# Gated-delta attention block on one Trainium2 core: the sums of squares of the queries are made once, from queries read back from DRAM during the inverse, and no longer in each recurrence unit

## The chip, the cores and the metric

The kernel runs on one core of one Trainium2 chip. The metric is the device time of one execution in microseconds (us). The engines are TensorE (PE, with its weight loads PEld), VectorE (DVE), ScalarE (ACT), GpSimd (POOL) and SyncE (SP), which here only issues transfers. Each engine works through its own instructions in order, and they are tied together by semaphores.

## The reference

The block is a modulated layer norm, a gated delta rule over 4 sequences of 512 tokens with 6 heads (key size 64, value size 128), a gated output norm and projection, and then a modulated feed-forward part. What matters for the change is cut out here:

```python
def short_conv(x, w):
    K = w.shape[1]
    xp = jnp.pad(x, ((0, 0), (K - 1, 0), (0, 0)))
    y = sum((xp[:, i:i + x.shape[1], :] * w[:, i] for i in range(K)))
    return jax.nn.silu(y)

def l2norm(x):
    return x * jax.lax.rsqrt(jnp.sum(x * x, -1, keepdims=True))

def _step(S, xs):
    qt, kt, vt, gt, bt = xs
    S = S * jnp.exp(gt)[..., None, None]
    pred = jnp.einsum('bhk,bhkv->bhv', kt, S)
    delta = (vt - pred) * bt[..., None]
    S = S + jnp.einsum('bhk,bhv->bhkv', kt, delta)
    return (S, jnp.einsum('bhk,bhkv->bhv', qt, S))
...
q = l2norm(q) * dk ** (-0.5)
k = l2norm(k)
...
o = o * jax.lax.rsqrt(jnp.mean(o * o, -1, keepdims=True) + EPS) * norm_weight
o = o * jax.nn.silu(gate)
```

The length of a query scales one row of `o`, and `o` is normalised afterwards. So the kernel leaves the queries as they are and adds their sum of squares, times 128 x EPS x 64, to the sum of squares of `o` before the root: this is the only place where the query's norm is used.

## The kernel before

The program is a list of steps (`plan`), built by plain Python; each engine then walks the list and issues its own part of each step. So the place of a step in the list sets the order on all five engines.

1. **Norms and the keys' projections** (to about 95 us). x is normed, turned and modulated into Hhi and Hlo (a value and its rest, for products of three matmuls each), and the decay, beta and key projections are made. The keys' sums of squares are made here: squares on ACT (`k2_square`), six matmuls with the selector `pick` for each half (`k2`, line 1121), a turn by PE, and further steps.
2. **Projections with the inverse beside them** (to about 340 us). 15 weight tiles in the order of `tile_seq`, each for 4 batches, make 60 slots. A slot issues one projection ahead (12 matmuls of 512 columns, four PSUM banks in turn). Tiles 0 to 2 are the queries, 3 to 8 the values: for these ACT scales the projection into one of two buffers Y (`conv_in`, line 1417), DVE adds three taps of the short convolution (`conv_tap`, line 1707), ACT applies SiLU into one of three buffers O (`conv_out`, line 1422), and SP stores the tile to the DRAM tensor `scrU` (`store_u`, line 933). Tiles 9 to 14 are the gates: ACT alone takes them to O (`gate`, line 1427). Beside the slots run three lanes of side work: one makes the matrices to be inverted (`inverse_1`) and later merges them, one does the 31 steps of the inverse on DVE (`inverse_2`: a multiply and an add for each, lines 1797 and 1800; two of these instructions in a convolution's slot, three in a gate's), one the late modulation rows. Side work that needs PSUM uses two pairs of banks in turn (`take`, `pfree`). POOL clears the four parts of P (`clear_p`, line 2016) for the inverse's results, which `inv2_back` loads at 275 us. P is 48 KB of each partition, in four parts: the first is used earlier for the products of `inv_gm`, the second and third by the inverse, the fourth for squares of keys.
3. **Recurrence** (to about 560 us). 16 units (a chunk of 64 tokens of two batches, 6 heads). A slot holds the recurrence of unit u, the preparation of u + 1, and the post-work of u - 1 and u - 2 (`slot_of`, line 650). SP loads the unit's queries and values from `scrU` into one of two buffers U. PE's order in a slot is `rec_x`, `pr_tr`, `pr_exp`, `rec_d`, `po_tr`, `pr_kq`, `rec_q`, `rec_s`, `rec_o`, `rec_v`, `po_wo`. POOL squares the unit's queries (line 2048, into Q2), PE sums them over the 64 rows of a head at the end of `pr_kq` (line 1227), DVE scales the sums into QN (line 1844), and the post-work adds QN to the squares of `o` (line 1879).
4. **Feed-forward part** (to the end), nearly all PE.

Three lines of the part that goes:

```python
for m in range(3):
    t = mm(bank(4 + 2 * p)[:, 192 + 2 * m:194 + 2 * m], Q2[:, m, :], halves, False, True)
t.then_inc(sem("pr_kq"), 1)
```

## Time and profile before

| | us |
|---|---|
| median of 3 runs | 1142.64 |
| lowest and highest run | 1140.72, 1145.05 |
| profiled execution, its own time | 1141.11 |
| its span in the trace | 1139.3 |
| PE busy | 1066.0 (94%) |
| DVE busy | 619.6 (54%) |
| ACT busy | 371.8 (33%) |
| POOL busy | 228.3 (20%) |

Read the busy shares as averages over stages with different limits. The granted clock of PE was 0.971 of full speed over the span. PE's busy time counts records that overlap, so the time that an instruction takes on PE is read from the distance of starts, not from its own length.

### The profile page before, as it was taken

To read this page: it belongs to the slowest core of one execution; us is meant where nothing else is said; L and a number is where in the kernel's file an instruction comes from. 1 tells how busy PE (TensorE), PEld (TensorE's weight loads), DVE (VectorE), ACT (ScalarE), POOL (GpSimd) and SP (SyncE) were. 2 spreads that over 40 slices of the span, in tenths; PEclk is the share of its full clock that TensorE was granted. 3 is DMA by queue.
4 is the path that set the end of the run, shared out by engine and by line. 5 is a ranking of instruction groups with operands and counts; after the bars stand their busy time and mean duration, and the time that the engine had idled before them with its cause. 6 is when DMAs were issued, how large, how long until landed. Compare 5 with 4: busy or idle time off the path is not lost.

```text
span 1139.3 us, 18747 instructions
## 1 busy us (share of the span) xinstructions
PE 1066.0 (94%) x7396; PEld 863.5 (76%) x7396; DVE 619.6 (54%) x994; ACT 371.8 (33%) x670; POOL 228.3 (20%) x182
## 2 busy tenths in 40 slices
PE   4898989988998999999978999999999999999998
PEld 2685667767776888888756788788888888888886
DVE  3766445998864677776645433333343334325356
ACT  4575465324435333343236112121121211212110
POOL 1322110001014555555331000000000000004092
PEclk8899999999898999999979999999999999999999
DMA  5503326338328455665622101001010000101222
GB/s 192 193 10 102 80 63 166 94 96 200 85 74 196 95 129 126 154 154 126 191 69 65 56 1 38 18 1 56 1 56 1 28 28 1 56 1 65 67 82 110
DMA packets 147350, 94.72 MB, mean 83 GB/s; under 512 B 93376, under 2 KB 124352, under 8 KB 147136
## 3 DMA queue, kind: packets, MB, share of 16 engines
...
## 4 chain that ended last, share of the span: by engine, by line
PE 79%; DVE 9%; ACT 5%; issue 4%; DMA 1%; POOL 1%; SPq 0%; DVEq 0%; ACTq 0%; POOLq 0%
PE ps L1051 75%; ACT t L1351 5%; PE ps L1059 3%; DVE t L1615 3%; DVE t L1707 3%; PE ps L1239 1%; DVE t L1620 1%; DMA t<-in_x 1%; POOL t L2081 1%; DMA t<-scrU 0%; ACT L1373 0%; DVE t L1807 0%; DMA t<-in_wf 0%; DVE t L1625 0%; DVE t L1818 0%
## 5 line engine op out<-in xcount | busy, mean ns | idle before, releaser
L1051 PE MATMUL ps<-t,t 128*128 128x512 f32 (+6 forms) x6528 | 1009.2, 337 | 55.4 <-DMA t<-in_wmod 8.7
L1051 PEld LDWEIGHTS ps<-t,t 128*128 128x128 f32 (+3 forms) x6528 | 803.5, 168 | 237.1 <-issue 43.1
L1615 DVE TENSOR_TENSOR t<-ps,t 128x512 f32<-128x512 f32 (+4 forms) x306 | 209.2, 701 | 255.0 <-PE ps L1051 243.1
L1351 ACT ACTIVATE t<-t 128x512 fp32r<-128x512 f32 (+7 forms) x330 | 185.0, 578 | 340.8 <-DVE t L1615 201.6
L1615 DVE TENSOR_TENSOR t<-t,t 128x512 fp32r<-128x512 f32 (+16 forms) x209 | 161.9, 779 | 116.6 <-ACT t L1351 109.5
L1351 ACT ACTIVATE t<-ps 128x512 f32<-128x512 f32 (+4 forms) x193 | 108.3, 566 | 329.8 <-PE ps L1051 317.0
L2089 POOL TENSOR_TENSOR t<-t,t 128x512 f32<-128x512 f32 x16 | 22.3, 1392 | 404.6 <-DVE t L1615 402.5
L1707 DVE SCALAR_TENSOR_TENSOR t<-ps,t,t 128x511 f32<-128x511 f32 (+2 forms) x108 | 80.4, 747 | 19.8 <-ACT t L1351 17.0
L1059 PE MATMUL ps<-t,t 128*128 128x128 f32 (+1 forms) x388 | 60.9, 292 | 11.9 <-DVE t L1620 8.9
L1351 ACT ACTIVATE t<-ps,t 128x512 f32<-128x512 f32 (+2 forms) x96 | 56.9, 621 | 33.3 <-DVE t L1615 10.7
L1059 PEld LDWEIGHTS ps<-t,t 128*128 128x128 f32 (+1 forms) x388 | 45.8, 149 | 28.0 <-DVE t L1620 12.8
L2069 POOL TENSOR_TENSOR t<-t,t 128x768 fp32r<-128x768 f32 x16 | 29.1, 1817 | 38.9 <-ACT t L1351 38.6
L2016 POOL MEMSET t<- 128x3072 f32 x4 | 10.7, 2666 | 123.0 <-DVE t L1615 92.9
L2092 POOL TENSOR_TENSOR t<-t,t 128x512 f32<-128x512 f32 x16 | 23.5, 1468 | 41.0 <-DMA t<-scrX 39.0
L1993 POOL TENSOR_TENSOR t<-t,t 128x512 fp32r<-128x512 f32 x16 | 21.2, 1324 | 50.9 <-ACT t L1351 49.1
L2075 POOL TENSOR_TENSOR t<-t,t 128x512 f32<-128x512 f32 x16 | 20.5, 1280 | 50.4 <-DVE t L1615 50.3
L1625 DVE BATCH_NORM_STATS2 t<-t 128x6 f32<-128x512 f32 x32 | 22.1, 690 | 13.2 <-DMA t<-in_x 8.4
L1351 ACT ACTIVATE t<-t,t 128x1 f32<-128x1 f32 (+2 forms) x36 | 13.2, 366 | 48.8 <-DVE t L1627 48.7
L2004 POOL TENSOR_TENSOR t<-t,t 128x384 f32<-128x384 f32 x16 | 14.0, 872 | 57.6 <-PE ps L1051 38.2
L1695 DVE SCALAR_TENSOR_TENSOR t<-ps,t,t 128x510 f32<-128x510 f32 (+1 forms) x24 | 17.9, 744 | 12.4 <-ACT t L1351 11.9
L2061 POOL TENSOR_TENSOR t<-t,t 128x768 f32<-128x768 f32 x16 | 23.6, 1474 | 2.7 <-POOL t L2075 2.4
L1620 DVE TENSOR_SCALAR t<-t,t,t 128x512 f32<-128x512 f32 x32 | 20.6, 645 | 0.6 <-ACT t L1351 0.6
...
## 6 DMA issues: line engine op xcount, KB each, us to landing
...
t<-in_x SPq DMA_DIRECT2D x32, 128.0 KB, 2.8
```

The source lines that it names most:

```text
L1051: return e.matmul(o, l, r_, start=start, stop=stop, skip_group_check=True)
L1059: return e.transpose(o, i, idn)
L1351: return e.activation(o, i, f, **kw)
L1615: return e.tensor_tensor(o, a, b, op)
L1620: return e.tensor_scalar(o, a, s1, s2, o1, o2)
L1625: e.bn_stats(st6[:, slot_, :], src).then_inc(sem(name + "bn"), 1)
L1707: e.scalar_tensor_tensor(yy[:, d + 1:SEQ], p_[:, 0:SEQ - d - 1], cwt[:, j, 2 - d:3 - d], yy[:, d + 1:SEQ], ALU.mult, ALU.add).then_inc(sem ...
L1993: signal(e.tensor_tensor(Hlo[:, b, k, :], HF[k][:, :], Hhi[:, b, k, :].bitcast(f32), ALU.subtract), "p_lo")
L2061: signal(e.tensor_tensor(heads(Sg[:, :, :]), heads(S[:, 6 * pp:6 * pp + 6, :]), bc(decay, 3, [128, 2, 3, 128]), ALU.mult), "p_sg")
L2069: signal(e.tensor_tensor(OZl[:, :, :], OZ[:, :, :], OZh[:, :, :].bitcast(f32), ALU.subtract), "p_ozl")
L2089: signal(e.tensor_tensor(ya(b, s), ya(b, s), gbB[:, b, :], ALU.mult), "p_out")
L2092: signal(e.tensor_tensor(ya(b, s), ya(b, s), xo(b, s), ALU.add), "p_out")
```

## The change

A fourth lane, `q_norms`, starts in slot 21 (the second slot of the sixth tile, after the last query tile has been given to the store). In that slot SP gets twelve loads, one for each of 3 query tiles and 4 batches, from `scrU` into places in the first and the fourth part of P (QS, QQ), and POOL two squares of 128 x 3072 in place. Three slots later, in slot 24, PE sums them with `pick` in twelve matmuls into four strips of one bank (`q_sum`) and ACT copies the bank to SBUF; in slot 25 PE turns the sums in sixteen small matmuls (`q_turn`) and ACT scales them into `q_eps` in eight instructions; in slot 26 POOL clears the fourth and the first part of P, which it did before in the ninth step of the inverse. `q_eps` is the tile of `beta`, whose last reader is over by then. Q2, QN, the square, the three matmuls and the scaling in each unit are gone. `inv2_back` waits for the clears by their new numbers.

```diff
--- before.py
+++ after.py
@@ -129,6 +129,10 @@
     tmp = A_.new([128, 768])
     K2 = [at(P_at[3] + i * 6144, [128, 3, 512]) for i in range(2)] + [A_.new([128, 3, 512])]
     kq = tmp[:, 0:512]
+    QS = [at(P_at[3], [128, 6, SEQ]), at(P_at[0], [128, 6, SEQ])]
+    QQ = [[QS[0][:, g_, :] for g_ in range(4)], [QS[1][:, g_, :] for g_ in range(4)],
+          [QS[g_ // 2][:, 4 + g_ % 2, :] for g_ in range(4)]]
+    qsum, q_eps = QQ[0][0], beta
     IG = [at(P_at[0] + i * 1536, [128, H, 64]) for i in range(8)]
     assert A_.p <= 229216, A_.p
 
@@ -168,8 +172,7 @@
     UG = [B_.new([128, H, 128]) for _ in range(2)]
     O2, OS, OZ = (B_.new([128, H, 128]) for _ in range(3))
     OZh, OZl = B_.new([128, H, 128], f32r), B_.new([128, H, 128], f32r)
-    Q2 = B_.new([128, 3, 128])
-    QN, ssq = B_.new([128, 2, H]), B_.new([128, 2, H])
+    ssq = B_.new([128, 2, H])
     rso = B_.new([128, H])
     XB = [B_.new([128, D]) for _ in range(2)]
     Woh = B_.new([128, H, D], f32r)
@@ -464,27 +467,46 @@
             made["kk"] = u + 1
             yield
 
+    cleared = {}
+
+    def clear(s):
+        step("clear_p", s=s)
+        cleared[s] = tick("p_pz")
+
+    def q_norms():
+        step("q_square")
+        yield
+        yield
+        yield
+        p, free = take()
+        step("q_sum", bank=4 + 2 * p, free=free)
+        pfree(p, ("a_k2c", 3))
+        yield
+        p, free = take()
+        step("q_turn", p=p, free=free)
+        pfree(p, ("a_k2", 3))
+        yield
+        clear(3)
+        clear(0)
+
     def inverse_2():
         yield
         step("inv2_load")
         for _ in range(4):
             yield
         for i in range(31):
-            if i == 8:
-                step("clear_p", s=3)
-                step("clear_p", s=0)
             step("inv2_mul", i=i)
             yield
             step("inv2_add", i=i)
             yield
-        step("clear_p", s=1)
+        clear(1)
         yield
         step("inv2_store")
-        step("clear_p", s=2)
+        clear(2)
         for _ in range(3):
             yield
         for s in range(4):
-            step("inv2_back", s=s)
+            step("inv2_back", s=s, cleared=cleared[s])
         for _ in range(3):
             yield
         made["inverse"] = 1
@@ -505,8 +527,8 @@
               (4, 2, inverse_1(3)), (0, 2, merge(0), "inverse", 1), (0, 2, merge(1)), (0, 2, merge(2)),
               (0, 2, merge(3))],
              [(0, 3, inverse_2(), "kk", 16)],
-             [(0, 1, late_mods())]]
-    running, left = [None] * 3, [0] * 3
+             [(0, 1, late_mods())], [(21, 1, q_norms())]]
+    running, left = [None] * 4, [0] * 4
     slot = 0
 
     def due(lane, now):
@@ -615,12 +637,12 @@
                 late_out.append((y, tap, tile, b))
             if n == 14:
                 start_b(b)
-            for l in (2, 0, 1):
+            for l in (2, 3, 0, 1):
                 side(l)
             slot += 1
     while any(running) or any(lanes):
         begin(99)
-        for l in range(3):
+        for l in range(4):
             side(l)
     n_proj = count["proj"]
     step("table", set="natural_log_exp_and_others")
@@ -948,6 +970,14 @@
                 blocks = scrA.rearrange("s b t i -> (s b) t i")
                 for i in range(3):
                     e.dma_start(nAp[:, i, :, :], blocks[128 * i:128 * i + 128]).then_inc(sem("d_nap"), 16)
+            elif kind == "q_square":
+                e.wait_ge(sem("inv_g"), 16)
+                e.wait_ge(sem("k2"), 2)
+                for m in range(3):
+                    for b in range(4):
+                        e.wait_ge(*at_least(stored[(m, b)]))
+                        src = scrU.rearrange("(s b) p j t -> b j p s t", b=4)[b, m]
+                        e.dma_start(QQ[m][b].rearrange("p (s t) -> p s t", s=4), src).then_inc(sem("d_cT"), 16)
             elif kind == "inv2_store":
                 e.wait_ge(sem("v_i2a"), 31)
                 blocks = scrP.rearrange("s b c t -> (s b) c t")
@@ -956,7 +986,7 @@
             elif kind == "inv2_back":
                 s = st["s"]
                 e.wait_ge(sem("d_pp"), 48)
-                e.wait_ge(sem("p_pz"), (2, 3, 4, 1)[s])
+                e.wait_ge(*at_least(st["cleared"]))
                 for k in range(4):
                     q = slice(32 * k, 32 * k + 32)
                     e.dma_start(P[q, s, :, q],
@@ -1126,6 +1156,21 @@
                 e.wait_ge(sem("a_k2c"), 2)
                 for i in range(4):
                     t = tr(bank(st["bank"])[:, 128 * i:128 * i + 128], kq[:, 128 * i:128 * i + 128], ident)
+                t.then_inc(sem("k2"), 1)
+            elif kind == "q_sum":
+                e.wait_ge(*at_least(st["free"]))
+                e.wait_ge(sem("p_q2"), 2)
+                for m in range(3):
+                    for g_ in range(4):
+                        t = mm(bank(st["bank"])[32 * g_:32 * g_ + 32, :], pick[:, m, :], QQ[m][g_], m == 0, m == 2)
+                t.then_inc(sem("k2"), 1)
+            elif kind == "q_turn":
+                e.wait_ge(*at_least(st["free"]))
+                e.wait_ge(sem("a_k2c"), 3)
+                for c in range(8):
+                    for half in range(2):
+                        t = mm(PSt[64 * half:64 * half + 64, 4 + 2 * st["p"] + c // 4, c % 4 * 128:c % 4 * 128 + 128],
+                               qsum[:, 64 * c:64 * c + 64], ident, c % 4 == 0, True)
                 t.then_inc(sem("k2"), 1)
             elif kind == "sums":
                 bk = bank(4 + 2 * st["p"])
@@ -1220,11 +1265,8 @@
                     for half in range(2):
                         for par in range(2):
                             q = slice(64 * par, 64 * par + 64)
-                            mm(PSt[64 * half:64 * half + 64, 4 + 2 * p + par, m * 64:m * 64 + 64],
-                               kcols(u)[q, m, 64 * half:64 * half + 64], U[u % 2][q, m, 64 * half:64 * half + 64], m == 0, True)
-                e.wait_ge(sem("p_q2"), u + 1)
-                for m in range(3):
-                    t = mm(bank(4 + 2 * p)[:, 192 + 2 * m:194 + 2 * m], Q2[:, m, :], halves, False, True)
+                            t = mm(PSt[64 * half:64 * half + 64, 4 + 2 * p + par, m * 64:m * 64 + 64],
+                                   kcols(u)[q, m, 64 * half:64 * half + 64], U[u % 2][q, m, 64 * half:64 * half + 64], m == 0, True)
                 t.then_inc(sem("pr_kq"), 1)
             elif kind == "rec_v":
                 u = st["u"]
@@ -1457,6 +1499,21 @@
                 rows = slice(64 * half, 64 * half + 64)
                 e.wait_ge(sem("k2"), half + 1)
                 act(kq[rows, :], bank(st["bank"])[rows, :], ACT.Copy).then_inc(sem("a_k2c"), 1)
+            elif kind == "q_sum":
+                e.wait_ge(sem("k2"), 4)
+                act(qsum, bank(st["bank"]), ACT.Copy).then_inc(sem("a_k2c"), 1)
+            elif kind == "q_turn":
+                e.wait_ge(sem("k2"), 5)
+                e.wait_ge(sem("v_br"), 1)
+                src = PSt[:, 4 + 2 * st["p"]:6 + 2 * st["p"], :].rearrange("p b (i c g m a) -> p g c (b i) a m", i=2, c=2, g=4, a=2)
+                dst = q_eps[:, :, :].rearrange("p (s v c) (a m) -> p v c s a m", s=4, v=2, a=2)
+                for half in range(2):
+                    rows = slice(64 * half, 64 * half + 64)
+                    for v_ in range(2):
+                        for c in range(2):
+                            t = act(dst[rows, v_, c], src[rows, 2 * v_ + half, c, :, :, 0:3], ACT.Copy,
+                                    scale=128.0 * EPS * DK)
+                t.then_inc(sem("a_k2"), 1)
             elif kind == "k2_log":
                 e.wait_ge(sem("v_k2"), 4)
                 act(z2[:, :, :], kq2[:, :, :], ACT.Ln).then_inc(sem("a_k2"), 1)
@@ -1839,11 +1896,6 @@
             elif kind == "pr_kq":
                 u, p = st["u"], st["p"]
                 e.wait_ge(sem("pr_kq"), u + 1)
-                if u >= 2:
-                    e.wait_ge(sem("v_ms"), u - 1)
-                e.tensor_scalar(QN[:, u % 2, :].rearrange("p (a m) -> p m a", a=2),
-                                bank(4 + 2 * p)[:, 192:198].rearrange("p (m a) -> p m a", a=2), 128.0 * EPS * DK, None,
-                                ALU.mult).then_inc(sem("v_qn"), 1)
                 e.wait_ge(sem("a_pexp"), u + 1)
                 if u >= 2:
                     e.wait_ge(sem("rec_o"), u - 1)
@@ -1875,8 +1927,8 @@
                     e.wait_ge(sem("a_pn"), 2 * u - 2)
                 e.tensor_reduce(ssq[:, u % 2, :], O2[:, :, :], mybir.AxisListType.X, ALU.add).then_inc(sem("v_red"), 1)
                 e.wait_ge(sem("v_red"), u + 1)
-                e.wait_ge(sem("v_qn"), u + 1)
-                tt(ssq[:, u % 2, :], ssq[:, u % 2, :], QN[:, u % 2, :], ALU.add).then_inc(sem("v_ms"), 1)
+                e.wait_ge(sem("a_k2"), 3)
+                tt(ssq[:, u % 2, :], ssq[:, u % 2, :], q_eps[:, u, :], ALU.add).then_inc(sem("v_ms"), 1)
             elif kind == "po_os":
                 u = st["u"]
                 e.wait_ge(sem("a_pn"), 2 * u + 2)
@@ -2002,16 +2054,19 @@
                 sh = [128, H, 64]
                 in_order()
                 signal(e.tensor_tensor(IG[u % 8][:, :, :], bc(later, 1, sh), bc(g[:, u, :], 2, sh), ALU.mult), "p_ig")
+            elif kind == "q_square":
+                e.wait_ge(sem("d_cT"), 16 + 12 * 16)
+                for q_ in QS:
+                    in_order()
+                    signal(e.tensor_tensor(q_[:, :, :], q_[:, :, :], q_[:, :, :], ALU.mult), "p_q2")
             elif kind == "clear_p":
                 s = st["s"]
-                if s == 0:
-                    e.wait_ge(sem("inv_g"), 16)
-                elif s == 1:
+                if s == 1:
                     e.wait_ge(sem("v_i2m"), 31)
                 elif s == 2:
                     e.wait_ge(sem("d_pp"), 48)
                 else:
-                    e.wait_ge(sem("k2"), 2)
+                    e.wait_ge(sem("k2"), 5)
                 in_order()
                 signal(e.memset(P[:, s, :, :], 0.0), "p_pz")
             elif kind == "clear_b":
@@ -2041,11 +2096,6 @@
                                        ALU.mult), "p_gm")
                 in_order()
                 signal(e.tensor_tensor(GMl[:, :, :], bc(within, 1, sh), bc(glo[:, u, :], 2, sh), ALU.mult), "p_gm")
-                e.wait_ge(sem(f"d_u{u % 2}"), 32 * (u // 2 + 1))
-                if u:
-                    e.wait_ge(sem("pr_kq"), u)
-                in_order()
-                signal(e.tensor_tensor(Q2[:, :, :], U[u % 2][:, 0:3, :], U[u % 2][:, 0:3, :], ALU.mult), "p_q2")
             elif kind == "rec_x":
                 u = st["u"]
                 pp = place(u)[0]
```

PE in the recurrence, the end of one slot's middle part. Before (t94 is a buffer U, t25 the keys kT, t1 the constants, t114 Q2, t89 the state S):

```order
1394 L1051 MATMUL ps<-t94_142,t25_73 64x64 [waits d_u1,v_prep]
1395 L1051 MATMUL ps<-t94_142,t25_73 64x64 x11
1396 L1051 MATMUL ps<-t1_49,t114_162 128x2 [waits p_q2]
1397 L1051 MATMUL ps<-t1_49,t114_162 128x2 x2
1398 L1051 MATMUL ps<-t89_137,t100_148 64x128 [waits v_os]
```

and with the change (t96 is U, t91 S):

```order
1387 L1081 MATMUL ps<-t96_144,t25_73 64x64 [waits d_u1,v_prep]
1388 L1081 MATMUL ps<-t96_144,t25_73 64x64 x11
1389 L1081 MATMUL ps<-t91_139,t102_150 64x128 [waits v_os]
```

The three matmuls on the squares and PE's wait for POOL's square (p_q2) are gone; nothing else in the slot moved.

ACT in slots 23 to 26 of the projections. Before (t37 to t39 are the buffers O, t35 and t36 the buffers Y, t32 a weight tile's upper part, t31 the next one's):

```order
203 L1351 ACTIVATE t39_87<-ps 128x512 [waits proj,d_scrU2]
204 L1351 ACTIVATE t32_80<-t30_78 128x512 [waits d_w1,proj]
205 L1351 ACTIVATE t35_83<-ps,t2_50 128x512 [waits a_cout,proj]
206 L1351 ACTIVATE t36_84<-ps,t2_50 128x512 [waits a_cout,proj]
207 L1351 ACTIVATE t37_85<-t35_83 128x512 [waits v_tap,d_scrU0]
208 L1351 ACTIVATE t35_83<-ps,t2_50 128x512 [waits a_cout,proj]
```

and with the change (t55 is the first of the squared tiles, whose first 512 columns take the sums, t9 is `q_eps`):

```order
205 L1393 ACTIVATE t35_83<-ps,t2_50 128x512 [waits a_cout,proj]
206 L1393 ACTIVATE t55_103<-ps 128x512 [waits k2]
207 L1393 ACTIVATE t36_84<-ps,t2_50 128x512 [waits a_cout,proj]
208 L1393 ACTIVATE t37_85<-t35_83 128x512 [waits v_tap,d_scrU0]
209 L1393 ACTIVATE t9_57<-ps 64x4x6 [waits v_br,k2]
210 L1393 ACTIVATE t9_57<-ps 64x4x6 x7
211 L1393 ACTIVATE t35_83<-ps,t2_50 128x512 [waits a_cout,proj]
```

The copy of the sums stands between the scalings (`conv_in`) of slots 24 and 25, the eight small instructions before that of slot 26.

SP after the change, from the slot before the lane starts (t56 is the second squared tile):

```order
98 L955 DMA scrU<-t39_87 128x4x128 [waits a_gate]
99 L955 DMA scrU<-t37_85 128x4x128 [waits a_gate]
100 L980 DMA t55_103<-scrU 128x4x128 [waits d_scrU0,k2,inv_g]
```

and after ten more loads:

```order
111 L980 DMA t56_104<-scrU 128x4x128 [waits d_scrU1]
112 L955 DMA scrU<-t38_86 128x4x128 [waits a_gate]
113 L955 DMA scrU<-t39_87 128x4x128 [waits a_gate]
114 L923 DMA t30_78<-in_W1 128x512 [waits v_wlo]
```

The stores 112 and 113 and the weight load 114 stood right behind 99.

## Rows read from the trace of the kernel before

**Rows 1.** The page, the chain that ended last, by engine.
```profile
PE 79%; DVE 9%; ACT 5%; issue 4%; DMA 1%; POOL 1%; SPq 0%; DVEq 0%; ACTq 0%; POOLq 0%
```

**Rows 2.** Busy us of PE, PEld, DVE, ACT, POOL by stretch; PE clock, DMA share, GB/s.
```profile
200.00:250.00 50.00, 44.20 (x190) 34.98 (x189) 48.51 (x64) 16.54 (x28) 0.00 (x0) 1.00 0.35 100
400.00:450.00 50.00, 50.00 (x603) 43.20 (x596) 34.39 (x58) 16.33 (x38) 26.56 (x23) 1.00 0.55 125
```

**Rows 3.** Order of time, PE in one unit: start us, us, engine, operation.
```profile
467.10 0.19 PEld L1051 LDWEIGHTS ps<-t,t 128*128 128x128 f32 x1
...
467.65 0.19 PEld L1051 LDWEIGHTS ps<-t,t 128*128 128x128 f32 x1
...
471.35 0.48 PE L1051 MATMUL ps<-t,t 128*128 128x512 f32 x1
```

**Rows 4.** The chain that ended last, in order of time: start us, us, what.
```profile
452.95 4.28 PE ps L1051 x90
...
466.66 4.27 PE ps L1051 x90
```

**Rows 5.** Order of time, POOL in the same unit.
```profile
468.61 1.82 POOL L2069 TENSOR_TENSOR t<-t,t 128x768 fp32r<-128x768 f32 x1 [2.79 <-ACT t L1351]
```

**Rows 6.** Groups by line and form: count, busy us, mean ns, idle before.
```profile
L2061 POOL TENSOR_TENSOR t<-t,t 128x768 f32<-128x768 f32 x16 | 23.6, 1474 | 2.7 <-POOL t L2075 2.4 <-POOL t L2048 0.2 <-POOL t L2030 0.2
...
L2016 POOL MEMSET t<- 128x3072 f32 x4 | 10.7, 2666 | 123.0 <-DVE t L1615 92.9 <-PE ps L1051 25.5 <-DMA scrP<-t 4.2
...
L1844 DVE TENSOR_SCALAR t<-ps 128x6 f32<-128x6 f32 x16 | 2.7, 167 | 8.6 <-PE ps L1051 8.6
```

**Rows 7.** Order of time, start of the recurrence, three engines.
```profile
362.05 0.83 POOL L2048 TENSOR_TENSOR t<-t 128x384 f32<-128x384 f32 x1 [5.54 <-DMA t<-scrU]
...
363.02 2.38 POOL L2030 TENSOR_TENSOR t<-t,t 128x1024 fp32r<-128x1024 f32 x1
...
364.00 1.41 DVE L1615 TENSOR_TENSOR t<-t,t 128x6 f32<-128x6 f32 x1
...
366.34 0.94 PE L1051 MATMUL ps<-t,t 128*128 128x128 f32 x6 [1.07 <-DVE t L1615]
```

**Rows 8.** Order of time, SP's queue: the third of the five stores.
```profile
202.40 0.67 SPq L933 DMA_DIRECT2D scrU<-t  x1
```

**Rows 9.** Order of time, ACT in slots 22 to 25.
```profile
204.47 0.60 ACT L1351 ACTIVATE t<-ps 128x512 f32<-128x512 f32 x1 [3.22 <-DMA scrU<-t]
205.26 0.60 ACT L1351 ACTIVATE t<-ps 128x512 f32<-128x512 f32 x1 [0.19 <-DMA scrU<-t]
...
209.16 0.69 ACT L1351 ACTIVATE t<-ps,t 128x512 f32<-128x512 f32 x1 [2.03 <-PE ps L1051]
```

**Rows 10.** DMA from 200 to 212 us, in 40 slices of 0.3 us.
```profile
GB/s 0 0 0 0 0 0 55 102 143 273 360 347 341 343 353 331 329 350 167 7 266 282 287 294 290 282 41 0 0 0 0 0 0 0 0 0 82 116 239 416
```

**Rows 11.** Order of time, PE: a modulation row, and a sum of keys' squares.
```profile
15.19 1.94 PE L1051 MATMUL ps<-t,t 128*32 128x512 f32 x8
...
85.43 2.77 PE L1051 MATMUL ps<-t,t 128*32 128x512 f32 x12
```

**Rows 12.** PE by the microsecond: length, busy, clock, DMA share, GB/s.
```profile
277.00:278.00 1.00, 0.41 (x2) 1.00 1.25 244
...
280.00:281.00 1.00, 0.00 (x0) 0.71 1.27 138
...
287.00:288.00 1.00, 1.00 (x5) 0.88 1.06 166
```

**Rows 13.** Order of time, slots 24 to 31: DVE, and PE's projections.
```profile
212.02 1.72 DVE L1615 TENSOR_TENSOR t<-t,t 128x660 f32<-128x660 f32 x2
...
213.65 2.31 DVE L1707 SCALAR_TENSOR_TENSOR t<-ps,t,t 128x511 f32<-128x511 f32 x3
...
223.94 13.92 PE L1051 MATMUL ps<-t,t 128*128 128x512 f32 x60 [0.96 <-DVE t L1707]
```

**Rows 14.** Groups by line and form: ACT's copies of merged blocks.
```profile
L1351 ACT ACTIVATE t<-ps 32x192 f32<-32x192 f32 x32 | 10.3, 321 | 31.6 <-PE ps L1051 31.2
```

## The prediction

> **What bounds the kernel now.** I read the chain first, then the stages, then the order of time at the two places that the change touches. The chain that ended last runs on TensorE (PE) for 79% of the span and on DVE for 9% [rows 1]. The reader is to see that this average hides two kinds of stage [rows 2]. From 400 to 450 us, in the recurrence, PE has 50.00 busy us in 50 and DVE 34.39: each PE instruction there is paid in full. From 200 to 250 us, where the projections run beside the inverse, DVE has 48.51 of 50 and PE 44.20: DVE sets the pace, and PE, ACT and POOL have slack only as long as none of them makes DVE wait. The change takes work out of the first and puts work, and waits, into the second.
>
> **What is removed.** In each unit PE sums the squares with three products (two records each) right after the 64x64 products of `pr_kq`. The first of their weight loads begins at 467.10 and the last, the sixth, at 467.65 [rows 3]: 0.11 us apart, so the next work could begin at 467.76. That is 0.66 us a unit. The groups of PE work return every 13.7 us (452.95, 466.66 [rows 4]), with PE never idle. Fifteen units in PE-bound slots give 15 x 0.66 = 9.9 us; the sixteenth, in the prologue, I cost at nothing and keep for the range.
>
> Does the next wait take it back? The nearest is that of `po_wo`, which starts at 471.35 [rows 3] and needs POOL's subtraction, 468.61 + 1.82 = 470.43 [rows 5]. The start moves to 470.69, and 0.26 us is left. So I expect the slot to shrink by the whole 0.66.
>
> POOL loses 16 squares of 0.83 us or more and DVE 16 scalings on 6 columns of 0.17 [rows 6]. Neither bounds a steady slot, so both cost nothing there. At the start it is different. A DVE add on as few columns took 1.41 us from 364.00 and ended with a POOL subtraction for Wo (363.02 to 365.40), and PE stood 1.07 us for DVE right after [rows 7]. POOL came that late because the square of unit 2 stood ahead of it, from 362.05 after 5.54 us of waiting for its queries. Without the square I take 1.1 us as gained (bounds 0 and 2). All that is gained: 11.0 us, from 9 to 13.
>
> The Trainium skill says of such a row, in "SBUF — State Buffer", section "Who interferes with whom", that a DVE instruction with two SBUF inputs and a GpSimd instruction that reads SBUF exclude each other for a whole instruction. By that rule the new squares would block steps of the inverse on DVE; by the times below DVE is already standing when the first square starts, so the sum stays as it is by row and rule alike, and were they to meet, the loss would be larger, not smaller.
>
> **What is added, step by step.** On SP twelve loads of 256 KB (3.1 MB) come between the third and the fourth of the five stores that now go out from 201.37.
>
> - *Issue.* The third store is issued at 202.40 and takes the queue 0.67 [rows 8]: the loads are issued from 203.07. What they wait for has happened by then, except the last query tile's store, which is the first of the three.
> - *Transfer.* The first two stores' landings let ACT go at 204.47 and 205.26 [rows 9]: 0.79 us for 256 KB, in the same pieces of 512 bytes, while up to 360 GB/s flow [rows 10]. The third lands at about 206.05, and twelve more at 0.79 make 9.5: 215.5. Bounds: 211.9, if only issue at some 0.57 each and 2 us to landing count; 216.8, at the 290 GB/s of the lower slices.
> - *Squares.* POOL starts when all twelve are in. It takes 0.83 us for 384 columns of the same operation, 1.47 for 768 and 2.38 for 1024 of others [rows 6, 7]: 2.16, 1.92 and 2.32 ns a column. Two squares of 3072 columns are 13.3 us at 2.16 (bounds 11.8 and 14.3). Ready at 228.8.
> - *`q_sum` on PE* stands behind slot 25's projection, which ends at 209.1, where ACT stops waiting for it [rows 9]. PE, in order, then stands until 228.8. Twelve products in four column strips follow. The six of a `k2` sum, in two strips, take 2.77 us, the four of a modulation row, in four strips, 1.94 [rows 11]: 0.46 and 0.48 each. Twelve make 5.5 (lower bound 2.8, if four strips go as fast as two).
> - *The clock.* PE went idle at 277.4; by 281 the granted clock had fallen from 1.00 to 0.50 (from 2.4 to 1.2 GHz), and it came back in the slice 287 to 288, some six microseconds after work had resumed [rows 12]. After 20 us of idle I expect the same: the first 6 us do 3 us of work. `q_sum` ends at 228.8 + 6 + 2.5 = 237.3.
> - *ACT* has the copy of the sums in its order ahead of the scaling that opens slot 25's convolution: 0.60 and 0.69 [rows 9] make 238.6. DVE needs that scaling at 213.65; before it stand only slot 24's taps and one step of the inverse [rows 13]. DVE waits 25.0 us.
> - *`q_turn`*, a slot later: PE's next projection, twelve products at 0.23 [rows 13], 2.8; sixteen products at 0.16, 2.5 (three full ones, as six records, take 0.94 [rows 7], and here two halves of the columns can share); eight small ACT instructions at 0.24, 1.9 (0.32 for 192 columns [rows 14], here 24); the next scaling, 0.7. 237.3 + 7.9 = 245.2. DVE would want it at 238.6 + 2.31 + 1.72 = 242.6. Another 2.6 us, from 0 to 4.
>
> Together DVE is 27.6 us later. Nothing absorbs it: DVE has no idle to give in this stage, the inverse stands behind the taps in DVE's own order, and PE is held by the same wait, so it can't run ahead. The stores behind the loads go out some 3 us late; the first buffer that they free is asked for at 216 in the old order, and if that cover fails it falls inside the long wait. POOL's clears of P now wait for `q_turn`, but the loads into P come at 275. Both cost nothing.
>
> For strips the Trainium skill ("TensorE: Matmul & The Clock Gate", "Why this matters for your kernels") gives a speed-up of 3.07 for four small tiles with different rows of the array and of 2.38 for three with different columns. By the latter, and 0.92 us a product in one strip, twelve would take 12 x 0.92 / 2.38 = 4.6 us, an estimate, and the sum would end 0.9 lower. I keep 5.5, since the row with four strips shows 0.48 a product.
>
> **Sum.** 27.6 - 11.0 = +16.6 us on the profiled execution's 1141.11: 1157.7, told as 1158. The median of the runs shown is 1142.64, 1.5 above that execution, and they spread over 4.3 us; the range covers it. About 0.5% (5.7 us) is what a measurement of this kernel can tell from no change.
>
> **Rivals.**
> - *The stall is hidden: faster.* With loads and squares done before DVE comes to 213.65 only the gain is left, 1130. Sum, clock and both ACT steps need at least 5.5 + 1.3, so the squares would have to end by 206.8, 3.7 us after the first load is issued. It decides there, and the DMA rows alone speak against it. Chance 0.04, with a half hidden one in it.
> - *The stall is short: no change.* POOL may run long instructions faster per column; its clears write 3072 columns in 2.67 us [rows 6]. At that pace both squares take 5.3, and at the other lower bounds the wait is 211.9 + 5.3 + 5.5 + 1.3 - 213.65 = 10.4 against a gain of 11: 1140.5, and 1143.5 with `q_sum` at 8.5. Against it: a clear reads nothing, and three operations that read agree on 1.9 to 2.3 ns. Chance 0.06.
> - *The gain fails: slower still.* `po_wo` has only 0.26 us left. If semaphores take more, PE waits there, and a gain under half leaves 1141.1 + 27.6 - 5 = 1164, or 1169 with none. Against it: POOL's subtraction hangs on `po_tr`, which does not move. Chance 0.10.
> - *Forecast*: full stall, full gain, 0.80.
>
> **How the numbers follow.** The low end of the stall is 211.9 + 11.8 + 5.5 + 1.3 - 213.65 = 16.9 with no second wait, and with a gain of 13 gives +4. The high end is 216.8 + 14.3 + 8.9 + 1.3 - 213.65 = 27.7 and a second wait of 4, with a gain of 9: +23. All at one end is rare; 8 in 10 reach from +7 to +26, the lower part of the failing gain among them: 1148 to 1167. Slower by over 0.5% holds the forecast and the failing gain, 0.90; within 0.5% the short stall, 0.06; faster 0.04.
>
> **What would show it.** Right: a hole on DVE and PE between about 210 and 238 us, ended by POOL's squares and then by ACT; two POOL instructions of about 6.6 us from 215; a clock of 0.50 behind the hole; slots of 13.0 us in place of 13.7, PE still at 50 of 50. Wrong: squares under 4 us each; a hole under 11 us; DVE time won back before 340, so that the recurrence starts less than 20 us later than now; slots that stay at 13.7, with PE waiting for POOL before `po_wo`.

## The result, and the profile after

The changed kernel takes 1151.11 us in the median of four runs (1149.09 to 1151.85), the kernel before, on the same chip, 1143.79 (1140.72 to 1145.05): a ratio of 1.0059, 95% interval 1.004 to 1.0078. It is **slower, by 0.6% or 7.3 us**. The direction was forecast and the median lies in the stated range, near its lower end; the size was not: +16.6 us forecast, less than half of it found. The profiled execution took 1149.09 us with a span of 1147.3, against 1141.11 and 1139.3.

The page of the changed kernel, the chain that ended last, by engine:

```profile
PE 74%; DVE 10%; ACT 6%; issue 4%; DMA 3%; POOL 2%; SPq 2%; DVEq 0%; ACTq 0%; POOLq 0%
```

PE has 5 points less of the chain than in [rows 1], and DMA, POOL and SP's queue, which were at 1, 1 and 0, now have 3, 2 and 2: the chain runs through the loads and the squares. The same two stretches as in [rows 2] (busy us of PE, PEld, DVE, ACT and POOL, then PE's clock, DMA share and GB/s), after:

```profile
200.00:250.00 50.00, 31.05 (x162) 22.36 (x161) 26.81 (x39) 11.20 (x26) 15.95 (x4) 0.80 0.44 116
400.00:450.00 50.00, 50.00 (x622) 43.25 (x621) 38.78 (x59) 18.33 (x40) 24.94 (x20) 1.00 0.56 126
```

Beside the inverse DVE lost 21.70 of its 48.51 busy us, and PE 13.15 of 44.20 (at a granted clock of 0.80, where it was 1.00). In the recurrence PE is full in both kernels, but does more of its instructions in the same time (622 against 603).

**The hole.** Order of time of the changed kernel, slots 24 to 26 (start us, us, engine, line, operation, and in brackets the idle time before it with what ended it). After the change the helpers' lines are L1081 for a product, L1393 for an ACT instruction, L1764 for the taps of a convolution and L1672 for the other DVE work:

```profile
203.64 10.04 SPq L980 DMA_DIRECT2D t<-scrU  x12
...
210.24 2.31 DVE L1764 SCALAR_TENSOR_TENSOR t<-ps,t,t 128x511 f32<-128x511 f32 x3
...
212.47 1.72 DVE L1672 TENSOR_TENSOR t<-t,t 128x660 f32<-128x660 f32 x2
...
218.29 10.69 POOL L2061 TENSOR_TENSOR t<-t 128x3072 f32<-128x3072 f32 x2 [73.22 <-DMA t<-scrU]
...
229.12 33.14 PE L1081 MATMUL ps<-t,t 128*32 128x512 f32 x170 [18.95 <-POOL t L2061]
...
234.10 0.60 ACT L1393 ACTIVATE t<-ps 128x512 f32<-128x512 f32 x1 [25.92 <-PE ps L1081]
...
235.31 2.32 DVE L1764 SCALAR_TENSOR_TENSOR t<-ps,t,t 128x511 f32<-128x511 f32 x3 [21.12 <-ACT t L1393]
...
238.97 0.85 ACT L1393 ACTIVATE t<-ps 64x24 f32<-64x24 f32 x8 [3.17 <-PE ps L1081]
239.84 0.69 ACT L1393 ACTIVATE t<-ps,t 128x512 f32<-128x512 f32 x1
...
240.56 2.32 DVE L1764 SCALAR_TENSOR_TENSOR t<-ps,t,t 128x511 f32<-128x511 f32 x3 [1.23 <-ACT t L1393]
```

Read down the brackets. POOL waited for the loads, PE 18.95 us for POOL, ACT 25.92 for PE, DVE 21.12 for ACT: one relay of four engines, each with its whole queue behind it. Slot 25's taps start at 235.31, where they started at 213.65 in [rows 13]; slot 26 adds a second, small wait of 1.23.

**Where it is given back.** Executions differ by some us in the stages before 210 us, so I compare distances between the same instructions. Four landmarks of the kernel before (slot 24's taps start at 209.79 in it), in order of time, are POOL's clear at the end of the merge and the fourth and sixteenth sum over a unit's squares in the recurrence:

```profile
331.80 1.38 POOL L2021 MEMSET t<- 128x1536 f32 x1 [54.08 <-PE ps L1051]
...
403.71 0.95 DVE L1876 TENSOR_REDUCE t<-t 128x6 f32<-128x768 f32 x1 [0.55 <-ACT t L1351]
...
566.15 0.94 DVE L1876 TENSOR_REDUCE t<-t 128x6 f32<-128x768 f32 x1
```

The same instructions of the changed kernel:

```profile
353.74 1.38 POOL L2076 MEMSET t<- 128x1536 f32 x1 [53.03 <-PE ps L1081]
...
421.55 0.95 DVE L1928 TENSOR_REDUCE t<-t 128x6 f32<-128x768 f32 x1
...
575.01 0.94 DVE L1928 TENSOR_REDUCE t<-t 128x6 f32<-128x768 f32 x1
```

| stretch | before, us | after, us | difference |
|---|---|---|---|
| slot 24's taps to the merge's last clear | 122.01 | 143.50 | +21.5 |
| that clear to the 4th sum (start of the recurrence) | 71.91 | 67.81 | -4.1 |
| 4th to 16th sum (steady slots) | 162.44 | 153.46 | -9.0 |
| all three | 356.36 | 364.77 | +8.4 |

Slot 24's taps start 0.45 us later than before in this pair, and 0.9 us is won behind the sixteenth sum; with these the span's +8.0 is complete. That last 0.9 may be chance: act_here below, with the same recurrence and the same end, takes 3.9 us longer than the change from there on.

### The profile page after: what moved, and what is told of

Its sections match the earlier page's. It is cut to its first block, busy times and chain, and to the rows that moved or that the text cites. A ratio compares the mean times of both kernels' runs of the same rounds, so it can differ in the third digit from the quotient of the medians.

```text
span 1147.3 us, 18633 instructions
## 1 busy us (share of the span) xinstructions
PE 1058.9 (92%) x7356; PEld 852.8 (74%) x7356; DVE 623.6 (54%) x978; ACT 372.1 (32%) x679; POOL 221.7 (19%) x168
## 4 chain that ended last, share of the span: by engine, by line
PE 74%; DVE 10%; ACT 6%; issue 4%; DMA 3%; POOL 2%; SPq 2%; DVEq 0%; ACTq 0%; POOLq 0%
PE ps L1081 70%; ACT t L1393 5%; DVE t L1672 4%; PE ps L1089 3%; DVE t L1764 3%; POOL t L2061 1%; PE ps L1281 1%; DMA t<-scrU 1%; DVE t L1677 1%; DMA t<-in_x 1%; POOL t L2131 1%; DMA t<-scrA 1%; ACT L1415 1%; SPq L980 1%; POOL t L2119 0%
## 5 line engine op out<-in xcount | busy, mean ns | idle before, releaser
L1081 PE MATMUL ps<-t,t 128*128 128x512 f32 (+5 forms) x6488 | 1001.2, 340 | 69.8 <-POOL t L2061 19.0
L1081 PEld LDWEIGHTS ps<-t,t 128*128 128x128 f32 (+3 forms) x6488 | 792.2, 167 | 254.9 <-issue 69.7
L1672 DVE TENSOR_TENSOR t<-ps,t 128x512 f32<-128x512 f32 (+4 forms) x306 | 208.2, 700 | 254.9 <-PE ps L1081 242.7
L1393 ACT ACTIVATE t<-t 128x512 fp32r<-128x512 f32 (+7 forms) x330 | 184.6, 577 | 329.1 <-DVE t L1672 202.3
L1393 ACT ACTIVATE t<-ps 128x512 f32<-128x512 f32 (+5 forms) x202 | 109.6, 551 | 352.8 <-PE ps L1081 339.9
L1672 DVE TENSOR_TENSOR t<-t,t 128x512 fp32r<-128x512 f32 (+16 forms) x209 | 162.3, 781 | 113.5 <-ACT t L1393 104.6
L1764 DVE SCALAR_TENSOR_TENSOR t<-ps,t,t 128x511 f32<-128x511 f32 (+2 forms) x108 | 80.4, 747 | 42.2 <-ACT t L1393 39.4
L1393 ACT ACTIVATE t<-ps,t 128x512 f32<-128x512 f32 (+2 forms) x96 | 56.8, 620 | 35.8 <-DVE t L1672 10.2
L2045 POOL TENSOR_TENSOR t<-t,t 128x512 fp32r<-128x512 f32 x16 | 21.2, 1326 | 51.9 <-ACT t L1393 50.2
L1393 ACT ACTIVATE t<-t,t 128x1 f32<-128x1 f32 (+2 forms) x36 | 13.2, 366 | 42.6 <-DVE t L1684 42.5
L1677 DVE TENSOR_SCALAR t<-t,t,t 128x512 f32<-128x512 f32 x32 | 26.3, 823 | 0.6 <-ACT t L1393 0.6
L2061 POOL TENSOR_TENSOR t<-t 128x3072 f32<-128x3072 f32 x2 | 10.6, 5306 | 73.3 <-DMA t<-scrU 73.2
L1752 DVE SCALAR_TENSOR_TENSOR t<-ps,t,t 128x510 f32<-128x510 f32 (+1 forms) x24 | 17.9, 744 | 12.4 <-ACT t L1393 11.8
```

The lines of the kernel that those rows point to most:

```text
L1081: return e.matmul(o, l, r_, start=start, stop=stop, skip_group_check=True)
L1393: return e.activation(o, i, f, **kw)
L1672: return e.tensor_tensor(o, a, b, op)
L1677: return e.tensor_scalar(o, a, s1, s2, o1, o2)
L1764: e.scalar_tensor_tensor(yy[:, d + 1:SEQ], p_[:, 0:SEQ - d - 1], cwt[:, j, 2 - d:3 - d], yy[:, d + 1:SEQ], ALU.mult, ALU.add).then_inc(sem ...
L2061: signal(e.tensor_tensor(q_[:, :, :], q_[:, :, :], q_[:, :, :], ALU.mult), "p_q2")
```

## The experiments

Each was run beside the kernel before on the same chip; ratios are to that kernel, with 95% intervals. The **main theory**: the time is the wait of slot 25 on the relay loads, squares, sum, copy, less the work that the recurrence no longer does, and the two add. Its main **rival**: something else of the change costs or gives, such as the DMA traffic, the moved memory, or a wait that a shorter slot uncovers. Lines left out of a diff are marked `...` or told below it.

### added_only: the change, with each unit's own squares and sums put back

```diff
+                e.wait_ge(sem("p_qu"), u + 1)
+                for m in range(3):
+                    t = mm(bank(4 + 2 * p)[:, 192 + 2 * m:194 + 2 * m], Q2[:, m, :], halves, False, True)
...
+                signal(e.tensor_tensor(Q2[:, :, :], U[u % 2][:, 0:3, :], U[u % 2][:, 0:3, :], ALU.mult), "p_qu")
```

> The change with the squares, the three sums and the scaling of each unit put back in the recurrence (the result of the new sums is computed and not used). Theory A, the wait at q_sum is the whole loss and it is passed on in full: the recurrence starts about 22 us later than in the kernel before, as in the change, and the time is 22 to 23 us above it (about 1165). Rival B, a good part of the hole is won back by slack before the end: under 15 us above it.

### gain_only: the kernel before, without the units' squares, sums and scalings

```diff
-                e.wait_ge(sem("p_q2"), u + 1)
-                for m in range(3):
-                    t = mm(bank(4 + 2 * p)[:, 192 + 2 * m:194 + 2 * m], Q2[:, m, :], halves, False, True)
...
-                signal(e.tensor_tensor(Q2[:, :, :], U[u % 2][:, 0:3, :], U[u % 2][:, 0:3, :], ALU.mult), "p_q2")
...
-                tt(ssq[:, u % 2, :], ssq[:, u % 2, :], QN[:, u % 2, :], ALU.add).then_inc(sem("v_ms"), 1)
+                tt(ssq[:, u % 2, :], ssq[:, u % 2, :], beta[:, u, :], ALU.add).then_inc(sem("v_ms"), 1)
```

> The kernel before without the unit's squares, sums and scaling, and nothing in their place: the output norm adds beta where the queries' sums belong. Theory A: the slot shrinks from 13.71 to 12.92 us as in the change, and with the start of the recurrence the time is 12 to 15 us below the kernel before (about 1129). Rival B, the change's slot was shorter for another reason (other placement of loads): the slot stays above 13.1 and the gain is under 9 us. Together with added_only: by A the two differences sum to that of the change, +7 to +8.

Measured: added_only 1164.45 us (1162.6 to 1168.79), ratio 1.0177 (1.014 to 1.0214), so +20.9 over the 1143.57 of the kernel before (22 to 23 were expected). gain_only 1128.14 us (1125.58 to 1133.45), ratio 0.986 (0.9821 to 0.99), so -15.4 (12 to 15 expected). Together +5.5, against the change's +7.3. The slot is 13.71 us in added_only, as before, and 12.92 in gain_only, as in the change. So the two halves add up to within two us, and the change is the difference of two larger effects, each with the sign that was forecast. The added half was overrated by 7 us (27.6 against 20.9), the removed one underrated by 4 (11.0 against 15.4). Part of those 15.4 is PE's clock: in the trace of gain_only, which is of its fastest run, it doesn't fall at the start of the recurrence, where it falls in the kernel before and in the change (rows further down).

### act_here: the change, with the squares on ACT, where POOL had them

```diff
         step("q_square")
-        yield
-        yield
-        yield
+        for _ in range(3):
+            yield
+        step("q_asq", i=0, n=12)
...
+            elif kind == "q_asq":
+                e.wait_ge(sem("d_cT"), 16 + 12 * 16)
+                for i in range(st["i"], st["i"] + st["n"]):
+                    q_ = QS[i // 6][:, i % 6, :]
+                    act(q_, q_, ACT.Square).then_inc(sem("a_q2"), 1)
```

(PE then waits for these twelve, and POOL has no squares.)

> The change with the squares on ACT, all twelve at once in slot 24 right before q_sum, nothing moved later. Theory: the hole is a serial sum of loads (until 218 us), squares, products and copies; ACT needs 12 x 0.6 = 7.2 us for the squares against POOL's 10.7, so the hole is 3.5 us shorter and the time 3 to 4 us below the change (about 1147). Rival: if the hole were set by something else than the end of the squares, the time stays at 1151.

Measured: 1146.27 us (1143.71 to 1151.69, ten runs), ratio 1.0028 (1.0009 to 1.0046). Order of time in it, the same places:

```profile
220.08 6.34 ACT L1393 ACTIVATE t<-t 128x512 f32<-128x512 f32 x12 [10.52 <-DMA t<-scrU]
...
226.57 13.73 PE L1081 MATMUL ps<-t,t 128*32 128x512 f32 x85 [15.79 <-ACT t L1393]
...
232.65 2.32 DVE L1769 SCALAR_TENSOR_TENSOR t<-ps,t,t 128x511 f32<-128x511 f32 x3 [16.38 <-ACT t L1393]
```

The squares take 6.34 us in place of 10.69, and DVE waits 16.38 us in place of 21.12: a link of the relay made 4.35 us shorter makes the wait 4.7 shorter. The time follows: the three stretches of the ledger sum to 360.06 us against the change's 364.77, 4.7 less. The medians stand 4.8 apart (the means 3.6, the runs of each kernel spread over up to 8), and the 1147 us expected was met. The squares' link is paid in full; the others were not varied.

### late12: the change, with the sum nine slots later

```diff
-        yield
-        yield
-        yield
+        for _ in range(12):
+            yield
         p, free = take()
         step("q_sum", bank=4 + 2 * p, free=free)
```

> The change with q_sum, q_turn and the two clears nine slots later (slots 33 to 35), loads and squares where they are. Theory A, only the wait cost: the hole at 210 to 235 is gone, and the time is 12 to 15 us below the kernel before (about 1129). Rival C, the squares of 5.3 us and the inverse's steps exclude each other on the port that POOL and DVE share (as the 1.41 us add of 6 columns did): single steps of the inverse on DVE take up to 5.3 us longer while a square runs, some 5 to 10 us in all, and the time is about 1135 to 1140. Rival D, the loads themselves hold up the stores: ACT waits for DMA before 220, several microseconds more than in the kernel before.

Measured: 1138.75 us (1134.42 to 1143.61, ten runs), ratio 0.9951 (0.9933 to 0.9969). The wait at slot 25 is gone, and yet not all of it comes back: from slot 24's taps to the merge's last clear it takes 133.31 us, 11.3 more than before. Theory A's 1129 us was missed, and rival C's 1135 to 1140 was met. (The profiled execution is the slowest of the ten, so its distances are read and not its end.) Order of time of late12:

```profile
222.00 11.24 POOL L2060 TENSOR_TENSOR t<-t 128x3072 f32<-128x3072 f32 x2 [76.30 <-DMA t<-scrU]
...
222.56 11.45 DVE L1671 TENSOR_TENSOR t<-t,t 128x720 f32<-128x720 f32 x2
...
233.93 2.30 DVE L1763 SCALAR_TENSOR_TENSOR t<-ps,t,t 128x511 f32<-128x511 f32 x3
```

The same two steps of the inverse in the kernel before:

```profile
219.81 1.84 DVE L1615 TENSOR_TENSOR t<-t,t 128x720 f32<-128x720 f32 x2
```

DVE's row counts as busy, but two steps that take 1.84 us take 11.45, just as long as POOL's two squares beside them: 9.6 us of the 11.3 lost without a wait in any list (the other 1.7 were not followed). This is what the Trainium skill describes in "SBUF — State Buffer", section "Who interferes with whom", for a DVE instruction with two SBUF inputs and a GpSimd instruction that reads SBUF, and this trace agrees. In the change itself DVE was standing already, as the prediction had it.

### late12_pieces: late12, with twelve squares of 512 columns

```diff
                 for q_ in QS:
-                    in_order()
-                    signal(e.tensor_tensor(q_[:, :, :], q_[:, :, :], q_[:, :, :], ALU.mult), "p_q2")
+                    for i in range(6):
+                        in_order()
+                        signal(e.tensor_tensor(q_[:, i, :], q_[:, i, :], q_[:, i, :], ALU.mult), "p_q2")
```

> As late12, with the two squares of 3072 columns cut into twelve of 512. Theory A: as late12. Rival C: a step of the inverse now waits for at most one piece of about 0.9 us, so this one is 3 to 8 us faster than late12. Should the squares get slower in pieces (a fixed cost for each), nothing waits for them before slot 33.

Measured: 1134.68 us (1133.2 to 1139.14), ratio 0.9921 (0.9892 to 0.995), 4.1 below late12, inside the 3 to 8 of rival C. Order of time:

```profile
221.76 17.66 POOL L2061 TENSOR_TENSOR t<-t 128x512 f32<-128x512 f32 x12 [75.16 <-DMA t<-scrU]
...
223.12 3.23 DVE L1671 TENSOR_TENSOR t<-t,t 128x720 f32<-128x720 f32 x2
...
228.49 20.20 DVE L1671 TENSOR_TENSOR t<-t,t 128x741 f32<-128x741 f32 x16
```

Now both engines suffer and neither stands long: POOL needs 17.66 us for 10.69 of work, and DVE 3.23 and 20.20 for what takes 1.84 and 14.77 undisturbed (act_late below shows both rows so). The merge's clear comes 126.49 us after slot 24's taps, 4.5 more than before. Pieces make the cost smaller, they don't remove it.

### act_late: the sum late, and the squares on ACT, two in each of six slots

```diff
-        yield
-        yield
-        yield
+        for _ in range(6):
+            yield
+        for i in range(0, 12, 2):
+            step("q_asq", i=i, n=2)
+            yield
...
         p, free = take()
         step("q_sum", bank=4 + 2 * p, free=free)
```

(`q_asq` and PE's wait as in act_here.)

> As late12, but the squares are made by ACT: twelve of 512 columns, two in each of slots 27 to 32; POOL has no square at all. Theory A' (what late12 and its pieces still lost, some 10 and 6 us against the 15 us of gain_only, was POOL's squares and DVE's steps of the inverse excluding each other): no step of the inverse is longer than 1 us, and the time is 13 to 15 us below the kernel before (about 1129). Rival D (the loss is the twelve loads in front of two stores, for which ACT waits until 222 us, or the extra work on PE): the time stays at the 1134 of late12_pieces or above.

Measured: **1129.27 us** (1126.31 to 1132.57), ratio 0.9868 (0.9839 to 0.9898). Nothing is left out of it, and it beats both kernels: 14.7 us under the 1144.01 of the kernel before, as theory A' had it. Order of time in it:

```profile
223.48 1.84 DVE L1681 TENSOR_TENSOR t<-t,t 128x720 f32<-128x720 f32 x2
...
224.78 2.18 ACT L1397 ACTIVATE t<-t 128x512 f32<-128x512 f32 x4
...
227.47 14.77 DVE L1681 TENSOR_TENSOR t<-t,t 128x741 f32<-128x741 f32 x16
```

DVE takes exactly what it took before, with ACT's squares beside it, and the windows show it at full work again:

```profile
200.00:250.00 50.00, 47.72 (x243) 37.10 (x242) 48.47 (x66) 23.13 (x49) 2.15 (x1) 1.00 0.61 164
```

DVE 48.47 busy us (48.51 before), and the clear at 122.19 (122.01 before). The twelve loads are as before in number and size, and DMA is busier than in the change (0.61 against 0.44), so the loads' traffic costs nothing that shows, and the moved memory, the same here, doesn't either: these parts of the rival fall. Against their own kernels before, gain_only gave 15.4 us and act_late 14.7: the added work, so placed, costs too little to be told from the spread of the runs.

### Which part of the gain is whose

Three kernels from the kernel before. no_pe_sum leaves out PE's sums and DVE's scaling, and keeps POOL's square (a unit's queries are then loaded only after the square that last read their buffer, which PE's sums had ensured before); no_pool_square leaves out the square, and PE sums the raw queries; sum_first leaves nothing out and only puts the sums ahead of the 64x64 products:

```diff
+                e.wait_ge(sem("p_q2"), u + 1)
+                for m in range(3):
+                    mm(bank(4 + 2 * p)[:, 192 + 2 * m:194 + 2 * m], Q2[:, m, :], halves, True, True)
                 for m in range(3):
                     for half in range(2):
...
-                e.wait_ge(sem("p_q2"), u + 1)
-                for m in range(3):
-                    t = mm(bank(4 + 2 * p)[:, 192 + 2 * m:194 + 2 * m], Q2[:, m, :], halves, False, True)
```

no_pe_sum:

> The kernel before without the three sums of squares on PE and the scaling on DVE; POOL still squares the queries of each unit, in the same place of its order (the output norm adds beta where the sums belong). Theory A: the slot is 12.92 us as in gain_only, so all of its 0.79 is PE's; the start of the recurrence gains nothing, and the time is 10 to 13 us below the kernel before, 1 to 4 above gain_only. Rival: if the slot stays above 13.1, part of the 0.79 was POOL's square.

no_pool_square:

> The kernel before with PE summing the queries themselves in place of their squares (the output norm gets sums without squares), and no square on POOL; PE's three products and DVE's scaling stay. Theory A: the slot stays at 13.7 us and only the start of the recurrence gains, 1 to 4 us (about 1140). Rival: a slot under 13.6, which would say that POOL's square held PE in every unit.

sum_first:

> The kernel before with the three sums of each unit moved ahead of the 64x64 products of pr_kq, behind the six turns of po_tr, which use the whole array too. Theory: the 0.79 us of the sums in a slot are six records at 0.11 and some 0.13 for one more change from whole-array to quarter-array products, since they stood between two groups of quarter-array products. Here that change is saved: the slot is 13.58 us in place of 13.71, 2 us over the recurrence. Rival: the 0.13 belongs to the records themselves, and the slot stays at 13.71. (A slot above 13.71 would say that PE now waits for the square or for the queries.)

| kernel | us (range) | ratio (95%) | slot | clear to 4th sum | PE's clock there | the two multiplied |
|---|---|---|---|---|---|---|
| before | 1143.57 to 1144.32 in three sets of runs | 1 | 13.71 | 71.91 | 0.95 | 68.3 |
| no_pe_sum | 1136.84 (1132.75 to 1139.09) | 0.9934 (0.9912 to 0.9956) | 12.92 | 71.85 | 0.95 | 68.3 |
| no_pool_square | 1142.29 (1140.63 to 1143.93) | 0.9983 (0.9971 to 0.9994) | 13.71 | 72.79 | 0.93 | 67.7 |
| gain_only (both) | 1128.14 (1125.58 to 1133.45) | 0.986 (0.9821 to 0.99) | 12.92 | 64.92 | 1.00 | 64.9 |
| the change | 1151.11 (1149.09 to 1151.85) | 1.0059 (1.004 to 1.0078) | 12.92 | 67.81 | 0.95 | 64.4 |
| sum_first | 1138.26 (1136.69 to 1141.69) | 0.995 (0.9933 to 0.9968) | 13.34 | 73.03 | 0.93 | 67.9 |

The slot is PE's alone: without the sums 12.92, without the square unchanged. The start of the recurrence is not so simple, and PE's clock has to be taken out of it first. PE by window, from the clear to the fourth sum (length, busy us, granted clock, DMA share, GB/s), before, in the change and in gain_only:

```profile
331.80:403.71 71.91, 65.45 (x794) 0.95 0.57 131
353.74:421.55 67.81, 61.81 (x765) 0.95 0.58 139
332.90:397.82 64.92, 58.85 (x765) 1.00 0.63 145
```

So of the 7.0 us by which gain_only is shorter than the kernel before, about half is a clock that didn't fall. Length times clock, the last column, is an estimate of the stretch at full clock. It gives 64.4 for the change and for act_here and late12_pieces too, 64.6 for late12 and 64.1 for act_late, though their clocks there go from 0.93 to 0.97, so it is a fair way to compare. By it nothing is won without the sums alone, 0.6 us without the square alone, and 3.4 to 3.9 without both.

Why the sums alone give nothing there, no_pe_sum's trace shows in order of time:

```profile
363.07 0.82 POOL L2040 TENSOR_TENSOR t<-t 128x384 f32<-128x384 f32 x1 [8.80 <-DMA t<-scrU]
...
375.09 7.61 PE L1052 MATMUL ps<-t,t 128*128 128x512 f32 x42 [5.93 <-POOL t L2061]
```

POOL stands 8.80 us at its square, for the loaded queries; two subtractions for Wo queue up behind it (4.84 us from 368.21), then the one that `po_wo` needs, and PE, early without its sums, stands 5.93 us for that. With the square gone too (gain_only), POOL makes the first of them at 358.17, and PE has no such wait. That is also why no_pe_sum came out 7.2 us below the kernel before and not the 10 to 13 expected. The slots expected of it and of no_pool_square, 12.92 and 13.7, were met, and so were no_pool_square's 1 to 4 us.

sum_first tells why the slot shrank by 0.79 and not by 0.66. (Its time is 6.1 us below the kernel before; 2 were expected. Its trace shows 4.1 of them, between the fourth and the sixteenth sum.) The PE work of one unit around the sums, in the chain in order of time (start us, us, what, with the count of records), is one group of 4.27 us in [rows 4], 3.92 in sum_first:

```profile
443.45 3.92 PE ps L1051 x90
...
456.79 3.92 PE ps L1051 x90
```

and 3.47 in the change:

```profile
455.21 3.47 PE ps L1081 x84
468.12 3.47 PE ps L1081 x84
```

The same 90 records take 0.35 us less if the six of the sum, which use the whole array, don't stand between two groups that use a quarter of it; the records themselves cost the other 0.45 (3.92 against 3.47). One of the two changes of form stands in the trace of the kernel before. The sixth weight load of the sums starts at 467.65 [rows 3], and the next work on PE is

```profile
467.86 0.67 PE L1051 MATMUL ps<-t,t 64*64 64x128 f32 x16
```

0.21 us later, where the six loads stand 0.11 apart. That the change of form is what costs is read from these distances; sum_first moved PE's wait for POOL's square as well, but PE has no idle there in either trace. Expected was 0.13, a slot of 13.58; it came to 13.34. The direction of the theory held and its size didn't.

## Why the prediction was right in direction and wrong in size

**The stall, by its steps.** Times after are less the 0.45 us by which this execution came to slot 24's taps later:

| step | forecast | measured |
|---|---|---|
| loads landed | 215.5 | 217.8 |
| two squares | 13.3 us | 10.8 |
| `q_sum`, with the slow clock | 8.5 us | 5.0 |
| ACT's copy and scaling | 1.3 us | 1.2 |
| DVE waits at slot 25 | 25.0 us | 21.2 |
| second wait, `q_turn` | 2.6 us | 1.3 |
| together | 27.6 us | 22.5 |

- *Issue and transfer*: 2.3 us too early. The queue took 10.04 us for twelve issues, 0.84 each. I took the pace of the stores in [rows 9]; for most of the time the loads ran at that of the slices around 290 GB/s, which I had only as the upper bound, 216.8, and ended even 1 us beyond it. The windows of PE by two microseconds show it, in the last column, while the clock falls from 0.75 to 0.50:

```profile
212.00:214.00 2.00, 0.00 (x0) 0.75 1.22 290
214.00:216.00 2.00, 0.00 (x0) 0.50 1.22 290
```

- *Squares*: 10.69 us for both, 1.74 ns a column where I took 2.16 from one with 384 columns, and below the lower bound of 11.8. This error and that of the loads cancel, by luck. The long instruction was cheaper per column than all three shorter ones that I read.
- *`q_sum` and its clock*: the step that failed most, 8.5 us where 5.0 were measured: the slow clock was paid twice. I took a product in four strips at 0.48 us from the modulation row of [rows 11], as if PE had been at full speed there, and then added 3 us for a halved clock. But PE ran at its slow pace in that row already. Lines by form (count of records, busy us, mean ns), of the modulation row, of the change's `q_sum` (1.2 GHz for most of it) and of late12's (2.4 GHz, nothing to wait for):

```profile
L1051 PE MATMUL ps<-t,t 128*32 128x512 f32 x8 | 1.9, 1062 | 0.0
...
L1081 PE MATMUL ps<-t,t 128*32 128x512 f32 x24 | 4.9, 986 | 19.0 <-POOL t L2061 19.0
...
L1080 PE MATMUL ps<-t,t 128*32 128x512 f32 x24 | 2.8, 596 | 0.0
```

  The view by window prints a clock of 1.00 at the modulation row, but four equal products right before it take 1.11 us, and 0.66 a little later:

```profile
14.15 1.11 PE L1059 MATMUL ps<-t,t 128*128 128x128 f32 x4 [1.11 <-DVE t L1620]
...
18.40 0.66 PE L1059 MATMUL ps<-t,t 128*128 128x128 f32 x4 [1.27 <-DVE t L1620]
```

  At full clock twelve products are 2.8 us, 0.23 each, half of the 0.46 with two strips: it was the lower bound of the prediction that held. The row with four strips shows the same at the slow pace, 0.48 a product. Of the two figures of the Trainium skill that were weighed ("TensorE: Matmul & The Clock Gate", "Why this matters for your kernels"), the one for different columns gave 4.6 (an estimate), and the 2.8 at full clock is less still. No run has a product in one strip, so the whole factor of four strips stays an estimate (0.92, twice the 0.46 with two strips, against 0.23). Twice 2.8 is 5.6, and the 5.0 come from the clock's return 4.3 us after work resumed, a little earlier than the six of [rows 12]:

```profile
232.00:233.00 1.00, 1.00 (x8) 0.50 0.00 0
233.00:234.00 1.00, 1.00 (x9) 0.77 0.00 0
234.00:235.00 1.00, 1.00 (x8) 1.00 0.00 0
```

  So four fifths of `q_sum` ran at 1.2 GHz: 3.9 us at 0.50 and 1 us at 0.77 are 2.7 us of full clock, which is the 2.8 of late12. Forecast were 8.5 us for 5.5 of full clock. act_late, where PE does not stand, has 1.00 from 200 to 250 us.
- *Second wait*: the eight ACT instructions of `q_turn` on 64x24 took 0.85 us together, where I took 0.24 each; sixteen products 2.0 us and not 2.5.
- *Nothing absorbs it*: right. At the merge's end 21.5 of the 22.5 us are left, and added_only shows 20.9 of them in the time of the whole.

**The gain.** 11.0 us forecast, 14.0 found (4.1 + 9.0 + 0.9), 15.4 alone. The steady slot gave 0.79 and not 0.66: I let the next work begin 0.11 us after the last of the six loads, at 467.76, and it began at 467.86, and the way into the sums had such a price too. The term of 1.1 us for the start was too small as a whole: the add on 6 columns now takes 0.17 us and not 1.41 [rows 7],

```profile
384.38 0.17 DVE L1672 TENSOR_TENSOR t<-t,t 128x6 f32<-128x6 f32 x1
```

but the start is shortened by 4.1. The same view of DVE divides them by the first, second and third sum, which come at 363.01, 374.16 and 390.00 in the kernel before and at

```profile
383.39 0.95 DVE L1928 TENSOR_REDUCE t<-t 128x6 f32<-128x768 f32 x1 [1.53 <-ACT t L1393]
...
393.02 0.95 DVE L1928 TENSOR_REDUCE t<-t 128x6 f32<-128x768 f32 x1 [1.34 <-ACT t L1393]
...
408.63 0.95 DVE L1928 TENSOR_REDUCE t<-t 128x6 f32<-128x768 f32 x1
```

in the changed one: 1.6 us up to the first, 1.5 between first and second, where the add is, 0.2 to the third and 0.8, a full slot's gain, to the fourth. So the 1.1 at the add were about right, and the 1.6 ahead of the first sum are of the prologue, whose sums on PE I had costed at nothing: the clock is about the same in both, and no_pool_square, which takes away the square alone, has at most 0.3 of them (32.72 us at a clock of 0.84, multiplied 27.5, against 31.21 at 0.89, 27.8).

**The rivals.** The stall is neither hidden nor short. What the short one builds on came half true, long squares that are cheaper per column and `q_sum` at its lower bound; the loads, later than forecast, kept the wait at 21.2. The gain did not fail, though it was close: 470.07 + 1.82 is 471.89, and `po_wo` starts at 472.03, 0.14 us later and with no idle before it.

```profile
470.07 1.82 POOL L2119 TENSOR_TENSOR t<-t,t 128x768 fp32r<-128x768 f32 x1 [2.79 <-ACT t L1393]
...
472.03 5.26 PE L1081 MATMUL ps<-t,t 128*128 128x512 f32 x42
```

**In sum**: at the merge's end the stall was 6.1 us smaller than forecast, the gain 3.0 larger, and 0.45 us of the traces' difference lie ahead of the change's place: 16.6 - 6.1 - 3.0 + 0.45 = 8.0. Both errors point the same way, so they add up. Of the signs that I had named, two of "wrong" came near: squares of 5.3 us where under 4 would have spoken for the short stall, and the recurrence's start, 20.4 us later by the first sum (19.9 by distance) but 17.8 by the fourth.
